# Attention and ternary FFN on one core: normalization on ScalarE, small statistics and the mean's term on GpSimd, the scores' masks as 64 by 64 products, new orders on every engine

## What is computed

```python
q, k, v = xn @ Wq, xn @ Wk, xn @ Wv          # 16 heads of 16
scores  = q . k over the 64 last tokens, * 16**-0.5, -inf before the start
ctx     = softmax(scores) @ v
attn    = ctx @ Wo
h       = gelu(xn @ absmean(W_fc).T)         # 1024 hidden
h       = layernorm(h) * ln_w + ln_b
ffn     = h @ absmean(W_proj).T              # absmean: ternary weights
out     = x + attn + ffn
```

## Time and profile before

| | us |
|---|---|
| three runs, median (lowest to highest) | 441.36 (438.65 to 442.75) |
| the profiled execution | 440.41 |
| its span | 438.6 |
| PE busy | 387.7 (88%) |
| DVE busy | 348.8 (80%) |
| ACT busy | 327.2 (75%) |
| POOL busy | 182.5 (42%) |

### The profile page before, as it was taken

How to read it: one execution, slowest core, us unless ns; L and a number is a source line. 1 busy time by engine, 2 the same in 40 slices (tenths; PEclk the granted TensorE clock), 3 DMA queues, 4 the chain that set the end, 5 groups by cost and what they waited for, 6 DMA issues and landing times.

```text
span 438.6 us, 13237 instructions
## 1 busy us (share of the span) xinstructions
PE 387.7 (88%) x5692; PEld 266.4 (61%) x5692; DVE 348.8 (80%) x679; ACT 327.2 (75%) x407; POOL 182.5 (42%) x110
## 2 busy tenths in 40 slices
PE   0389699799999999899989999899989998898885
PEld 0236256466656677467656677567755766666674
DVE  7977687597887799589968899689958997669864
ACT  2234179868896788778897789778896889779861
POOL 2700003546163262437154344427244716335851
PEclk9999799999998999999999999999999999999999
DMA  7119207900392009700591029400880049001002
GB/s 272 63 42 121 67 3 99 141 3 1 67 120 57 14 29 129 124 13 17 91 150 24 13 58 128 95 13 28 119 133 16 1 92 120 22 13 50 16 31 67
DMA packets 30682, 29.19 MB, mean 67 GB/s; under 512 B 5664, under 2 KB 29280, under 8 KB 30624
## 3 DMA queue, kind: packets, MB, share of 16 engines
q1 hardware_dynamic: 30624, 28.35, 39.0%
HBM read 7.35 MB, written 4.19 MB: 26 GB/s over the span
## 4 chain that ended last, share of the span: by engine, by line
PE 37%; DVE 21%; SPq 17%; DMA 16%; issue 5%; ACT 3%; POOL 1%; POOLq 0%; DVEq 0%; ACTq 0%
SPq L330 12%; DMA x_in<-in_x 10%; PE small L1049 9%; PE big L989 7%; DMA k_stack<-qk_split 6%; DVE negmax L691 5%; PE big L963 3%; PE small L1060 3%; SPq L345 3%; PE big L1008 3%; PE big L1002 3%; DVE y_bufs L730 3%; PE small L1076 2%; DVE g_lo L685 2%; DVE ctxn L741 2%
## 5 line engine op out<-in xcount | busy, mean ns | idle before, releaser
L429 POOL TENSOR_TENSOR p_parts<-probs,p_parts 128x1024 f16<-128x1024 f32 x64 | 137.1, 2154 | 93.3 <-ACT p_parts L539 93.3
L538 ACT ACTIVATE probs<-big,exp_scale 128x1024 f32<-128x1024 f32 x64 | 71.5, 1117 | 29.9 <-PE big L1032 29.8
L691 DVE TENSOR_REDUCE negmax<-big 128x8 f32<-128x1024 f32 x64 | 77.1, 1221 | 7.6 <-PE big L1008 6.7
L539 ACT ACTIVATE p_parts<-big,exp_scale 128x1024 f16<-128x1024 f32 x64 | 71.5, 1117 | 0.0
L1049 PE MATMUL small<-proj_t,g_hi 128*128 128x256 f16 x256 | 59.2, 278 | 0.2 <-DVE ctxn L741 0.2
L1049 PE MATMUL small<-proj_t,g_lo 128*128 128x256 f16 x256 | 58.8, 276 | 0.0
L989 PE MATMUL big<-fc_t,xt_hi 128*128 128x512 f16 x128 | 49.8, 389 | 3.0 <-DVE negmax L691 2.8
L989 PE MATMUL big<-fc_t,xt_lo 128*128 128x512 f16 x128 | 49.5, 387 | 0.0
L516 ACT ACTIVATE gel<-big 128x1024 f32<-128x1024 f32 x32 | 32.7, 1024 | 20.9 <-PE big L989 20.2
L685 DVE SCALAR_TENSOR_TENSOR g_lo<-big,lnw_s,g_hi 128x512 f16<-128x512 f32 x64 | 44.9, 742 | 0.1
L553 ACT ACTIVATE g_hi<-big,lnw_s 128x512 f16<-128x512 f32 x64 | 39.6, 690 | 2.4 <-PE big L1039 2.3
(11 more groups left out here) (130 smaller groups left out, 833.5 us busy)
## 6 DMA issues: line engine op xcount, KB each, us to landing
q_stack<-qk_split SPq DMA_DIRECT2D x48, 128.0 KB, 4.7
k_stack<-qk_split SPq DMA_DIRECT2D x48, 128.0 KB, 7.5
x_in<-in_x SPq DMA_DIRECT2D x8, 512.0 KB, 9.3
out<-y_bufs SPq DMA_DIRECT2D x32, 128.0 KB, 1.8
v_odd<-v_even SPq DMA_DIRECT2D x16, 132.0 KB, 4.8
v_odd<-v_even SPq DMA_DIRECT2D x16, 99.0 KB, 4.7
gel<-in_w_fc SPq DMA_DIRECT2D x1, 1024.0 KB, 7.1
y_bufs<-in_w_proj SPq DMA_DIRECT2D x1, 1024.0 KB, 8.9
```

Source lines behind the costliest of these rows:

```text
L429: g.tensor_tensor(p_lo[:, j % PB], probs[:, j % PB], p_hi[:, j % PB], ALU.subtract).then_inc(*sig(p_lo_ready))
L538: s.activation(probs[:, j % PB].rearrange("p i (u q) -> p u i q", u=2), st, ACT.Exp, scale=exp_scale[:, 0:1]).then_inc(*sig(exp_ready))
L539: s.activation(p_hi[:, j % PB].rearrange("p i (u q) -> p u i q", u=2), st, ACT.Exp, scale=exp_scale[:, 0:1]).then_inc(*sig(p_hi_ready))
L691: v.tensor_reduce(negmax[:, :, j], slot[b, "sa", j][:].rearrange("p a (u k) -> p (a u) k", k=P), AX.X, ALU.max, negate=True).then_inc(*sig ...
```

## The change

1. `normalize` moves from VectorE (subtract, multiply) to ScalarE: `Identity` with `scale=rstd` and `bias=nmr`, where `nmr = -mean * rstd`.
2. GpSimd's `token_rstd` makes `nmr` and `veps` as well: four instructions for one.
3. The hidden statistics move to GpSimd: `hidden_moments` (five small instructions), and `rs2` in `hidden_rstd`.
4. The mean's term moves to GpSimd: `add_mean` makes `csum * nrm2` for all four token tiles in `mean_term` and adds it to `res`. `add_projection` keeps one instruction, and waits before its first for `rs2_ready` and `mean_added`.
5. `sa` makes its masks in four 64 by 64 products for two of 64 by 128.
6. `fill_stacks` moves from VectorE to GpSimd, in u32 pairs, behind its constants, one buffer after the other.
7. The ring of probability buffers runs on over the batches: index `(b * NJ + n) % PB` for `n % PB`.
8. All orders are new: TensorE's, SyncE's, GpSimd's, ScalarE's and VectorE's, with a start, a period of three (two on VectorE) and an end written out. The four `gelu` of a batch stand in one run with only a `context_upper` between them, the exps in another; x of batch 1 is loaded right behind the weights.

The helper `wait(eng, b, name, n)` becomes `eng.wait_ge(*at(b, name, n))`, the same wait.

```diff
             def token_rstd(b):
-                wait(pool, b, veps_ready, 1)
-                g.tensor_tensor(rstd[:], veps[:], expo[:], ALU.pow).then_inc(*sig(rstd_ready))
+                pool.wait_ge(*at(b, ln_step, 2))
+                if b > 0:
+                    pool.wait_ge(*at(b - 1, xn_ready, 1))
+                g.tensor_scalar(nmr[:], mv[:, :, 0], -1.0, None, ALU.mult).then_inc(*sig(rstd_step))
+                g.tensor_scalar(veps[:], mv[:, :, 1], LN_EPS, None, ALU.add).then_inc(*sig(rstd_step))
+                pool.wait_ge(*at(b, rstd_step, 2))
+                g.tensor_tensor(rstd[:], veps[:], expo[:], ALU.pow).then_inc(*sig(rstd_step))
+                pool.wait_ge(*at(b, rstd_step, 3))
+                g.tensor_tensor(nmr[:], nmr[:], rstd[:], ALU.mult).then_inc(*sig(rstd_ready))
...
+            def add_mean(b):
+                pool.wait_ge(*at(b, rstd2_ready, 1))
+                pool.wait_ge(*at(b, res_ready, 1))
+                g.tensor_tensor(nrm2[:], mean2[:], rstd2[:], ALU.mult).then_inc(*sig(mean_step))
+                pool.wait_ge(*at(b, mean_step, 1))
+                g.tensor_tensor(mean_term[:], csum[:, 0:1, :].broadcast_to([P, NT, D]),
+                                nrm2[:].unsqueeze(2).broadcast_to([P, NT, D]), ALU.mult).then_inc(*sig(mean_step))
+                pool.wait_ge(*at(b, mean_step, 2))
+                g.tensor_tensor(res[:], res[:], mean_term[:], ALU.add).then_inc(*sig(mean_added))
...
+            def fill_stacks():
+                for i in range(2):
+                    step(g.memset(k_stack[:, i].bitcast(u32), MAX_UNIT_PAIR))
+                    g.memset(k_stack[:, i, :, 0:W].bitcast(u32), 0).then_inc(stacks_filled, 1)
+                    pool.wait_ge(stacks_filled, i + 1)
...
+            def normalize(b):                      # ScalarE
+                if b > 0:
+                    act.wait_ge(*at(b - 1, xt_done, 1))
+                act.wait_ge(*at(b, rstd_ready, 1))
+                for t in range(NT):
+                    last = s.activation(xn[:, t], x_in[:, b % 2, t], ACT.Identity, bias=nmr[:, t:t + 1],
+                                        scale=rstd[:, t:t + 1])
+                last.then_inc(*sig(xn_ready))
...
             def add_projection(b, t):
                 if t == 0:
-                    wait(dve, b, res_ready, 1)
+                    dve.wait_ge(*at(b, rs2_ready, 1))
+                    dve.wait_ge(*at(b, mean_added, 1))
                 v.scalar_tensor_tensor(out=y_ffn[:, b % 2, t], in0=slot[b, "proj", t][:, 0:D], scalar=rs2[:, t:t + 1],
                                        in1=res[:, t], op0=ALU.mult, op1=ALU.add).then_inc(*sig(proj_added))
-                wait(dve, b, proj_added, t + 1)
-                v.scalar_tensor_tensor(out=y_ffn[:, b % 2, t], in0=csum[:, 0], scalar=nrm2[:, t:t + 1],
-                                       in1=y_ffn[:, b % 2, t], op0=ALU.mult, op1=ALU.add).then_inc(*sig(ffn_ready))
...
                     for u in range(2):
                         rows = slice(u * W, (u + 1) * W)
-                        mm(ps[:, u], onehot[rows, 0:2].rearrange("p a q -> p (a q)"),
-                           mask_q[rows, 1 if n == 0 else 0].rearrange("p u k -> p (u k)"), start=True, stop=False)
+                        for a in range(2):
+                            mm(ps[a * W:(a + 1) * W, u], onehot[rows, a],
+                               mask_q[rows, 1 if n == 0 else 0].rearrange("p u k -> p (u k)"), start=True, stop=False)
```

More of the change, by code:

```diff
@@ new lines, in _ @@
+            hidden_moments(0)
+            residual(0)
+            lower_part(0, 0)
+            lower_part(0, 1)
+            lower_part(0, 2)
+            hidden_rstd(0)
+            add_mean(0)
+            token_rstd(2)
+            lower_part(0, 3)
+            lower_part(0, 4)
+            lower_part(0, 5)
+            lower_part(0, 6)
+            hidden_moments(1)
+            lower_part(0, 7)
+            residual(1)
+            lower_part(1, 0)
+            lower_part(1, 1)
+            lower_part(1, 2)
@@ new lines, in _ @@
+            lower_part(4, 5)
+            lower_part(4, 6)
+            hidden_moments(5)
+            lower_part(4, 7)
+            residual(5)
+            lower_part(5, 0)
+            lower_part(5, 1)
+            lower_part(5, 2)
+            hidden_rstd(5)
+            add_mean(5)
+            token_rstd(7)
+            lower_part(5, 3)
+            lower_part(5, 4)
+            lower_part(5, 5)
+            lower_part(5, 6)
+            hidden_moments(6)
+            lower_part(5, 7)
+            residual(6)
@@ new lines, in _ @@
+            lower_part(6, 0)
+            lower_part(6, 1)
+            lower_part(6, 2)
+            hidden_rstd(6)
+            add_mean(6)
+            lower_part(6, 3)
+            lower_part(6, 4)
+            lower_part(6, 5)
+            lower_part(6, 6)
+            residual(7)
+            lower_part(6, 7)
+            hidden_moments(7)
+            hidden_rstd(7)
+            add_mean(7)
+            lower_part(7, 0)
+            lower_part(7, 1)
+            lower_part(7, 2)
+            lower_part(7, 3)
@@ new lines, in _ @@
+            scale_context(0, 0)
+            statistics(2)
+            scale_context(0, 1)
+            maximum(1, 0)
+            add_projection(0, 0)
+            maximum(1, 1)
+            maximum(1, 2)
+            maximum(1, 3)
+            add_projection(0, 1)
+            maximum(1, 4)
+            scale_context(0, 2)
+            maximum(1, 5)
+            add_projection(0, 2)
+            scale_context(0, 3)
+            xt_lower(2)
+            maximum(1, 6)
+            maximum(1, 7)
@@ new lines, in _ @@
+            gelu_lower(1, 5)
+            v_lower(2)
+            gelu_lower(1, 6)
+            gelu_lower(1, 7)
+            context_lower(0, 1)
+            scale_context(1, 0)
+            statistics(3)
+            maximum(2, 0)
+            scale_context(1, 1)
+            add_projection(1, 0)
+            maximum(2, 1)
+            maximum(2, 2)
+            maximum(2, 3)
+            add_projection(1, 1)
+            maximum(2, 4)
+            scale_context(1, 2)
+            add_projection(1, 2)
@@ new lines, in _ @@
+            v_lower(6)
+            gelu_lower(5, 6)
+            gelu_lower(5, 7)
+            scale_context(5, 0)
+            context_lower(4, 1)
+            statistics(7)
+            maximum(6, 0)
+            scale_context(5, 1)
+            add_projection(5, 0)
+            maximum(6, 1)
+            maximum(6, 2)
+            maximum(6, 3)
+            add_projection(5, 1)
+            maximum(6, 4)
+            scale_context(5, 2)
+            add_projection(5, 2)
+            maximum(6, 5)
@@ L1023, in job @@
                     if n == 0:
-                        wait(pe, b, maxima_loaded, 4)
+                        pe.wait_ge(*at(b, maxima_loaded, 4))
                     for u in range(2):
```

837 lines of the change are left out of this document (600 added, 237 removed), and 43 rows, old and new, of tables (FIRST, LAST, PERIOD).

## The result

The changed kernel takes 400.73 us (median of four runs, 400.5 to 401.96), the kernel before, run beside it, 441.36 (median of three, 438.65 to 442.75; a fourth, at 447.28, lies over 1.5% above the fastest, counts as a slow run and is left out). The ratio is 0.9094, 95% interval 0.9036 to 0.9152: faster, inside the range, and 6.3 us faster than the forecast of 407. The profiled execution took 400.63, its span is 398.5, and it is 40.1 us shorter than the span before. In it PE is busy 373.4 us (94%), DVE 279.6 (70%), ACT 322.0 (81%), POOL 235.6 (59%).

A forecast was written before the change was run, and what follows sets the result against it. TensorE was taken to bound the middle, busy 46.0 of 48 us. Start -12.0, six periods -13.8, last batch to `st 0` -6.2 and end -1.4 sum to -33.4, from 440.41 to 407.0 us; range 399 to 419.

The forecast's parts named there:

- six periods: Middle, `sa 0` of batch 1 to batch 7: 45.8 us each, 274.8 where 288.6 stood, -13.8 us.
- `sa 0` to `st 0` of batch 7: Last batch: jobs moved elsewhere and shorter masks, with 1.7 us of gaps, 24.0 us for 30.2, -6.2.
- The start: Up to `sa 0` of batch 1: fill on GpSimd, transposes 5.8 us earlier, 73.4 us where 85.42 stood, -12.0.
- Rival 4: Start gains nothing, by a slow GpSimd memset or stacking DMAs still setting `sa 0`: +6 to +8, 414 us; chance 0.08.
- The masks: TensorE's `sa`: 64 by 64 products stream side by side, 0.10 us saved per job; 0.9 us per period with shape changes.
- Rival 2: Masks' column halves go one after the other on TensorE: 0.22 us more on 64 jobs, 421 us; chance 0.04.
- The gaps: TensorE's waits at hand-overs in the middle: 0.7 us left per period instead of 2.0.
- the case with gaps near nil: Everything covered better than on paper, TensorE's gaps near nil: 395 to 400 us; chance 0.05.
- Rival 1: TensorE keeps 2.0 us of gaps per period: 12 us lost over seven periods and the start, 419 us; chance 0.2.
- rival 3: Slow GpSimd multiply delays `mean_added`, VectorE and TensorE wait at `proj 0`: 455 at 13 us; chances 0.02 partly, 0.03 beyond 1% slower.

The follow-up runs named there:

- paired order: Changed kernel with `st 1` right behind `st 0` in six batches and the mask tiles' DMAs ahead of the first stacking DMAs: 403.95 us.

## Why the prediction was right, and where it was off

| | forecast | measured |
|---|---|---|
| start, to `sa 0` of batch 1 | 73.4 | 75.14 |
| six periods | 274.8 | 267.9 |
| `sa 0` to `st 0` of batch 7 | 24.0 | 22.9 |
| end | 33.0 | 32.6 |
| outside the span | 1.8 | 2.1 |
| time | 407.0 | 400.6 |

**The start.** Right up to the last link: fill until 9.1 (8.96), transposes at 13.0 (13.22), `qk 0` at 17.2 (17.81), `sa 0` at 39.3 (39.30), `st 0` at 57 (57.62). The 1.7 us that are missing came after it. TensorE's granted clock was 0.63 from 64.35 to 69.00, and in the five kernels without that stretch `sa 0` of batch 1 came 34.15 us after that of batch 0 for 35.84. The prediction had no term for the clock after a wait. Rival 4, a start that gains nothing, falls.

**The masks.** Right: two column halves side by side, 0.24 us to the products, 0.98 us per period for 0.9 by the experiment. Rival 2 falls. In the kernel before the same edit is worth 2.4 us in all, and its gaps grew by what TensorE saved: the term was right to be put into the new layout.

**The gaps** were the term that was mis-sized. I left 0.7 us per period for hand-overs with 0.1 to 0.9 us of slack on paper; there are 0.05. Six periods give 3.9 us of the 6.9 by this. The work itself is 44.8 us, not 46.0 - 0.9 = 45.1: another 1.9. The first period is 43.56, 1.3 short of the others, which I counted whole. `sa 0` to `st 0` of batch 7, with 1.7 us of gaps in the forecast, was 1.1 shorter, likely for the same reason. A hand-over with 0.1 us of slack waits for nothing when durations repeat (the middle periods are all 44.84 or 44.85); the paired order shows the other side, 0.4 us too little and a gap in each period. The forecast was right in its range and its direction, but the time came near its lower edge, and the case with gaps near nil, which is what happened, had a chance of 0.05: too little for an order whose every slack came out positive. Rival 1, gaps as before, falls.

**GpSimd.** `add_mean` is 4.6 us and the multiply 1893 ns, for 5.2 and 2.5: the residual's row was a bound from above. `add_mean` ended 1.8 us ahead of the first `add_projection` (209.82, 211.62), and by the experiment with three multiplies 2.6 us could be added; I had 1.0. The mechanism of rival 3 is real, its condition wasn't met. Its sum of 29 was 27.8.

**ScalarE.** The four Identity take 592 ns each by the records but 2.06 us together, for 1.9; table loads are 8 for gelu, 8 for exp, two per batch as forecast; 39.4 us for 39.5. **VectorE** 32.5 for 32.

**The ports that VectorE and GpSimd share.** Here the reason was half right. I expected the trace to go against the rule of the Trainium skill (Perfetto Trace Analysis, Optimizing Scalar/DVE Operations) that moving work between the two "might not help". The move helped: the stretched instructions were moved away, and what VectorE has left reads PSUM or, like the token statistics, isn't held. But the mechanism behind the rule made the largest difference that any experiment here shows, and I used it only for one instruction. I gave the normalization 1.6 us of VectorE's time (460 ns each) and no effect on TensorE. That price holds only for the place it had. At another place of the new order it costs 31 us (431.65 for 400.73), and with the small statistics and the mean's term there as well 65.

**What the parts are worth.** None of the sum's terms shows that they depend on each other. Alone, the moved work with the old orders, masks and fill is 445.08, and the new orders, masks and fill with the old division of work are 440.11, or 465.37 by the place of one call; together they give 400.73. The moved work takes from VectorE what GpSimd holds up, and with it gone the order keeps without gaps. Whether the old division could do so too with its small statistics and the mean's term at better places wasn't tried. From the changed kernel backwards the single parts are worth: masks 6.9 us, the mean's term on GpSimd 4.7, the fill on GpSimd 4.0, the normalization on ScalarE 2.1 with the best place on VectorE that I tried. The second and the fourth come from kernels whose start had the full clock, so at the same clock they are about 6.4 and 3.8, an estimate.

## What to carry to other kernels

Lay a period's jobs end to end with durations from the trace: where every hand-over comes out positive, expect no gaps rather than some. Before you move a VectorE instruction of a kind that was held here, look at what GpSimd does at that moment; the price of its old place says nothing of the new one, and a swap of two calls was worth 29 us. Here the moved work paid only with an order made anew for it, and the order only with the work that would be held up out of the way, so cost the two together. Before you credit an edit with a microsecond or two, compare the granted clock of the same stretch in both traces.

## What the hardware showed that I had not expected

- VectorE's TENSOR_SCALAR on SBUF and its SCALAR_TENSOR_TENSOR with two SBUF inputs are held to the end of GpSimd's instruction even when they are small: 2.27 and 1.98 us for 128x4 elements (0.17 and 0.16 alone), 4.99 us for four of 128x256 (1.38 alone). BATCH_NORM_STATS2 from SBUF to SBUF isn't held: 0.41 us beside a GpSimd add.
- After a wait of 3.17 us TensorE's granted clock was 0.65 over 4.8 us, after one of 1.6 us 0.63 to 0.68 over 4.65 in four kernels and 1.00 in six. The low stretch cost 1.7 us: a wait can cost more than its length.
- GpSimd's multiply with two broadcast operands takes 1893 ns at 128x1024 in fp32, its add of two full ones 2353.
